# A gather shared out between four engines: 75 instead of 46 of 832 columns leave GpSimd, and their offsets shrink to 16 bits

## The reference

```python
x = x + _L0_gnn_ref(h, ...)   # GCN: sum over edges of H[src] * norm
x = x + _L1_gnn_ref(h, ...)   # SchNet: sum over edges of h[src] * filter(edge)
x = x + _L2_gnn_ref(h, ...)   # 4 EdgeConv layers: max over edges
x = x + _L3_gnn_ref(h, ...)   # GCN twice: sum over edges
```

## Time and profile before

| | us |
|---|---|
| median of 3 runs | 9450.62 (9448.05 to 9455.34) |
| the profiled execution | 9444.14 |
| its span | 9442.3 |
| GpSimd busy | 6987.7 (74%) |
| VectorE busy | 3654.1 (39%) |
| ScalarE busy | 3485.0 (37%) |
| TensorE busy | 1819.4 (19%) |

### The profile page before, as it was taken

One profiled execution on the slowest core, in us unless ns is written; L12 is line 12 of the kernel. 1 busy time (PEld: TensorE's weight loads), 2 busy tenths in 40 slices (PEclk: granted clock), 3 DMA queues, 4 the chain that ended last, 5 costly groups with the idle time before them and its releaser, 6 DMA issues. The chain is left out here.

```text
span 9442.3 us, 137452 instructions
## 1 busy us (share of the span) xinstructions
PE 1819.4 (19%) x9607; PEld 1531.1 (16%) x9607; DVE 3654.1 (39%) x20408; ACT 3485.0 (37%) x23810; POOL 6987.7 (74%) x6815
## 2 busy tenths in 40 slices
PE   2000057788884000020002000020002000020000
PEld 1000046777774000010001000010001000010000
DVE  4333344444443333333333333333334333333333
ACT  4444221111114444334442444334442444324441
POOL 5777668888883777777777777777776777777777
PEclk6555567777777555565556555565555555555555
DMA  6444535555553333333333333333334333333333
GB/s 214 161 159 158 190 79 77 77 77 77 75 72 111 108 108 112 110 108 108 113 111 111 111 109 108 113 105 112 108 110 138 103 117 111 109 108 110 108 112 128
DMA packets 483882, 1071.04 MB, mean 113 GB/s; under 512 B 162484, under 2 KB 293278, under 8 KB 428104
## 3 DMA queue, kind: packets, MB, share of 16 engines
q0 software_dynamic: 310432, 442.95, 21.5%
q1 hardware_dynamic: 169557, 619.06, 17.8%
q10 hardware_dynamic: 2940, 1.00, 0.1%
HBM read 511.83 MB, written 559.14 MB: 113 GB/s over the span
## 5 line engine op out<-in xcount | busy, mean ns | idle before, releaser
L1035 POOL DMA_INDIRECT WORK<-table,S x5502 | 5194.3, 944 | 1923.2 <-issue 1689.0
L1071 DVE COPY FE<-XF 128x4 uint8 x9856 | 1311.1, 190 | 3271.9 <-issue 1824.8
L1114 ACT COPY FE<-XF 128x4 uint8 x20608 | 2101.3, 191 | 1104.6 <-issue 1092.0
L1134 ACT COPY WORK<-psum 128x512 f32<-128x512 f32 (+1 forms) x1456 | 846.3, 581 | 2874.1 <-DVE psum L1089 2864.6
L1304 POOL DMA_INDIRECT acc<-TOT,stage x832 | 1301.3, 1564 | 274.6 <-issue 209.7
L1089 DVE SCALAR_TENSOR_TENSOR psum<-psum,RESET,WORK 128x128 f32<-128x128 f32 x3320 | 1189.1, 358 | 493.3 <-DMA WORK<-table,S 426.8
L1154 PE MATMUL psum<-ident,FE 128*128 128x128 f32 x238 | 106.5, 447 | 6110.0 <-ACT FE L1114 4714.0
L1089 DVE SCALAR_TENSOR_TENSOR psum<-psum,KEEP,WORK 128x128 f32<-128x128 f32 x2490 | 896.9, 360 | 639.9 <-DMA WORK<-table,S 278.8
L1154 PEld LDWEIGHTS psum<-ident,FE 128*128 128x128 f32 x238 | 43.3, 182 | 6172.5 <-issue 5903.0
L1438 ACT COPY TOT<-psum 128x512 f32<-128x512 f32 x208 | 121.9, 586 | 1250.2 <-DMA acc<-TOT,stage 1245.0
L1509 DVE SCALAR_TENSOR_TENSOR BASE<-psum,WEIGHT,BASE 128x128 f32<-128x128 f32 x832 | 234.1, 344 | 761.9 <-PE psum L1379 761.8
(11 more groups left out here) (255 smaller groups left out, 2540.4 us busy)
## 6 DMA issues: line engine op xcount, KB each, us to landing
run_rows<-WORK SPq DMA_DIRECT2D x357, 1024.0 KB, 4.2
WORK<-table SPq DMA_DIRECT2D x10752, 0.5 KB
WORK<-table,S POOLq DMA_INDIRECT x5502, 2.6
fill_rows<-BASE SPq DMA_DIRECT2D x52, 1024.0 KB, 6.8
WORK<-fill_rows SPq DMA_DIRECT2D x104, 512.0 KB, 3.7
table<-TF SPq DMA_DIRECT2D x56, 384.0 KB
WORK<-carry_rows SPq DMA_DIRECT2D x49, 384.0 KB, 6.6
acc<-TOT,stage POOLq DMA_INDIRECT x832, 3.3
```

Source lines behind the costliest of these rows:

```text
L1035: pool.indirect_dma_start(RING_T[:, b * WIDE + k, :], None, table, table_row(table, INDEX[:, t:t + 1]))\
L1071: i = dve.tensor_copy(PICKED[:, s, e:e + 1].bitcast(u8), TT[:, ds(held_rows["dve"][e % 32], 4)])
L1114: i = act.copy(PICKED[:, j % 2, e:e + 1].bitcast(u8), TT[:, ds(held_rows["act"][e % 32], 4)])
L1134: act.copy(RING_T[:, t % SPAN:t % SPAN + n, :], CHAINED[:, t % PSUM_COLS:t % PSUM_COLS + n, :])\
```

## The change

The shares and their places are new: ScalarE takes 36 columns, VectorE 24, SyncE 15. The offsets of ScalarE's and VectorE's columns are unsigned 16-bit numbers in `ROWB`; SyncE's stay 32 bits wide in a tensor of their own, `ROWS`. ScalarE picks a unit of 32 edges in three of four quads, VectorE 4 edges at each column. SyncE's columns lie at place 14 of chunks 3, 6, 9, 12, 16, 19, 22, 25, 28, 32, 35, 38, 41, 44 and 48; the halves are fetched behind the stores of chunks c-3 and c-2.

```diff
-BY_ACT = [t for t in range(60, 772, 32)]
-BY_DVE = [t for t in range(108, 772, 64)]
-BY_SP = [t for t in range(84, 800, 64)]
+UNIT = 32
+UNITS = P // UNIT
+TT_LAST = 800
+ACT_QUADS = [q for q in range(3, TT_LAST // QUAD) if q % 4 != 3]
+BY_ACT = [t for t in (QUAD * (q + 3) for q in ACT_QUADS[UNITS - 1::UNITS]) if t < TT_LAST]
+STEP_EDGES = 4
+DVE_STEPS = P // STEP_EDGES
+BY_DVE = list(range(DVE_STEPS + 3 * QUAD + 1, TT_LAST, DVE_STEPS))
+SP_BLOCKS = [c for c in range(3, TT_LAST // WIDE) if c % 16 in (3, 6, 9, 12, 0)]
+BY_SP = [WIDE * c + WIDE - 2 for c in SP_BLOCKS]
...
-EDGES = 16
-X_BLOCK = 48
-STEP_EDGES = 2
+X_BLOCK = 50
...
-        ROWB = sb("ROWB", [len(AWAY), P], i32)
+        ROWB = sb("ROWB", [len(FROM_TT), P], u16)
+        ROWS = sb("ROWS", [len(BY_SP), P], i32)
...
+                    if t < QUAD or j >= len(BY_DVE):
+                        return
...
+                    if first % UNIT == 0:
+                        offsets["dve"] = row_offsets(mybir.EngineType.DVE, ROWB, len(BY_ACT) + j, first // UNIT)
+                    for e in range(first, first + STEP_EDGES):
...
+                    rows = row_offsets(mybir.EngineType.Activation, ROWB, j, unit)
+                    for e in range(UNIT):
+                        i = act.copy(PICKED[:, j % 2, unit * UNIT + e:unit * UNIT + e + 1].bitcast(u8),
+                                     TT[:, ds(rows[e], 4)])
...
-                        k = after - max(c - RING, -1)
-                        parts_of = ((0, 64), (64, 64)) if c >= RING else ((0, 128),)
-                        if not 0 <= k < len(parts_of):
+                        half = after - (c - RING + 1)
+                        if half not in (0, 1):
                             continue
...
+                        wait(sp, stored[c % RING], c // RING * 16 if half == 0 else 0)
+                        for unit in range(half * UNITS // 2, (half + 1) * UNITS // 2):
+                            rows = row_offsets(mybir.EngineType.SP, ROWS, j, unit, 4 * F)
```

More of the change, by code:

```diff
@@ L83, in gnn_kernel @@
     f32, i32, u32, bf16 = mybir.dt.float32, mybir.dt.int32, mybir.dt.uint32, mybir.dt.bfloat16
-    u8 = mybir.dt.uint8
+    u8, u16 = mybir.dt.uint8, mybir.dt.uint16
     ALU = mybir.AluOpType
@@ L632, in _ @@
                                   ALU.is_equal).then_inc(hot, 1)
-                for k, (t, size) in enumerate([(t, 4) for t in BY_ACT + BY_DVE] + [(t, 4 * F) for t in BY_SP]):
-                    i = dve.tensor_single_scalar(AWAY_F[:, k:k + 1], SRCF[:, t:t + 1], float(size), ALU.mult)
+                k = 0
+                for cols_of, period, size in ((BY_ACT, 3, 4), (BY_DVE, 1, 4), (BY_SP, 5, 4 * F)):
+                    n = len(cols_of)
+                    for r in range(period):
+                        own = cols_of[r::period]
+                        assert own == list(range(own[0], own[-1] + 1, own[1] - own[0]))
+                        i = dve.tensor_single_scalar(AWAY_F[:, k + r:k + n:period],
+                                                     SRCF[:, own[0]:own[-1] + 1:own[1] - own[0]],
+                                                     float(size), ALU.mult)
+                    k += n
                 i.then_inc(hot, 1)
@@ L650, in _ @@
                 st.did(dve.memset(CHAIN[:], 0.0))
-                st.did(dve.tensor_copy(ROWB[:], bank(0)[0:len(AWAY), P:2 * P]))
+                st.did(dve.tensor_copy(ROWB[:], bank(0)[0:len(FROM_TT), P:2 * P]))
+                st.did(dve.tensor_copy(ROWS[:], bank(0)[0:len(BY_SP), 2 * P:3 * P]))
                 st.join()
@@ L743, in _ @@
                 pe.wait_ge(hot, 3)
-                nc.tensor.transpose(bank(0)[0:len(AWAY), P:2 * P], AWAY_F, ident[:])
+                nc.tensor.transpose(bank(0)[0:len(FROM_TT), P:2 * P], AWAY_F[:, 0:len(FROM_TT)], ident[:])
+                nc.tensor.transpose(bank(0)[0:len(BY_SP), 2 * P:3 * P], AWAY_F[:, len(FROM_TT):len(AWAY)], ident[:])
                 nc.tensor.matmul(bank(7)[:, 0:NT], upper[:], deg[:], start=True, stop=True)
@@ L995, in _, with row_offsets @@
                 wait(sp, x_parked, 16 * NG if x_loads == 1 else 0)
-        def row_offsets(engine, k, first, n, size=4):
+        def row_offsets(engine, rows, k, unit, size=4):
             return nc.values_load_multi_w_load_instructions(
-                ROWB[k:k + 1, first:first + n], engines=[engine], min_val=0, max_val=(N_PAD - 1) * size,
+                rows[k:k + 1, unit * UNIT:(unit + 1) * UNIT], engines=[engine], min_val=0,
+                max_val=(N_PAD - 1) * size,
                 skip_runtime_bounds_check_because="the offsets are made of node numbers below N_PAD")[1]
@@ L1024, in passing @@
             tt_quads = pieces(NT, QUAD) if FROM_TT else []
-            held_rows = {}
+            offsets = {}
             def pool_part(pool):
@@ L1059, in pick_edges @@
                 def pick_edges(t):
[L1060 to L1074, removed]
+                    j, first = divmod((t - QUAD) * STEP_EDGES, P)
+                    if t < QUAD or j >= len(BY_DVE):
+                        return
+                    s = 2 + j % 2
+                    if first == 0:
+                        wait(dve, tt_copied, len(tt_quads) if j == 0 else 0)
+                        wait(dve, off_turned, FROM_TT.index(BY_DVE[j - 2]) + 1 if j > 1 else 0)
+                    if first % UNIT == 0:
+                        offsets["dve"] = row_offsets(mybir.EngineType.DVE, ROWB, len(BY_ACT) + j, first // UNIT)
+                    for e in range(first, first + STEP_EDGES):
+                        i = dve.tensor_copy(PICKED[:, s, e:e + 1].bitcast(u8),
+                                            TT[:, ds(offsets["dve"][e % UNIT], 4)])
+                    if first + STEP_EDGES == P:
+                        i.then_inc(built_v, 1)
                 for t in range(T):
@@ L1104, in pick_edges @@
                 def pick_edges(q):
[L1105 to L1117, removed]
+                    if q not in ACT_QUADS:
+                        return
+                    j, unit = divmod(ACT_QUADS.index(q), UNITS)
+                    if j >= len(BY_ACT):
+                        return
+                    if unit == 0:
+                        wait(act, off_turned, FROM_TT.index(BY_ACT[j - 2]) + 1 if j > 1 else 0)
+                    rows = row_offsets(mybir.EngineType.Activation, ROWB, j, unit)
+                    for e in range(UNIT):
+                        i = act.copy(PICKED[:, j % 2, unit * UNIT + e:unit * UNIT + e + 1].bitcast(u8),
+                                     TT[:, ds(rows[e], 4)])
+                    if unit == UNITS - 1:
+                        i.then_inc(built_a, 1)
                 for q, (t, n) in enumerate(tt_quads):
@@ L1173, in fetch @@
                         c = col // WIDE
-                        k = after - max(c - RING, -1)
-                        parts_of = ((0, 64), (64, 64)) if c >= RING else ((0, 128),)
-                        if not 0 <= k < len(parts_of):
+                        half = after - (c - RING + 1)
+                        if half not in (0, 1):
                             continue
[L1178 to L1184, removed]
+                        wait(sp, stored[c % RING], c // RING * 16 if half == 0 else 0)
+                        for unit in range(half * UNITS // 2, (half + 1) * UNITS // 2):
+                            rows = row_offsets(mybir.EngineType.SP, ROWS, j, unit, 4 * F)
+                            for e in range(UNIT):
+                                p = unit * UNIT + e
+                                sp.dma_start(RING_T[p:p + 1, col % SPAN, :].bitcast(u8),
                                              flat_table[:, ds(rows[e], 4 * F)]).then_inc(fetched[j % 2], 16)
@@ L1188, in sp_part @@
                     sp.wait_ge(blanked, 1)
-                fetch(-1)
                 for c in range(COUNT):
```

## The result

The changed kernel takes **13774.01 us** (median of 4 runs, 13770.05 to 13775.10) against 9449.33 for the kernel before, run beside it: a ratio of 1.4575, 95% interval 1.4549 to 1.4600. The range for 8 in 10 ended at 9700.

What follows compares the result with a forecast made beforehand. SyncE's loop was taken to bound the kernel instead of GpSimd's gathers: six passes +14 us and the first +70, together +84 on 9444.14, with the median 6.5 above, gave 9535 us; own range 9470 to 9650, 8 in 10 from 9330 to 9700.

Steps and rivals of the forecast that it cites:

- halves: SyncE's 128 row loads per column, in two groups of 64 behind chunk stores: 27.8 us each from store to store.
- The range for 8 in 10: Total time of the changed kernel expected between 9330 and 9700 us with 8 in 10 confidence.
- the price of the 16-bit register load: ScalarE's load of 32 registers from 16-bit offsets: between 1.0 and 3.9 us, taken at 1.978.
- hidden: ScalarE's 16.4 us per 16 columns stay below GpSimd's 18.0, except three times a pass.
- Register loads make ScalarE the bound: Rival: past 3.1 us a load, ScalarE exceeds 19.5 us per chunk; at 3.9, some 10400 us in all. Chance 0.05.
- SyncE's loop: Store, half, store, half, landing, reduce, lift, next store, where SyncE's chunks stand three apart: 59.1 us for 48 columns.
- ordinary pass: Each of six passes after the first: last gather at 982.6 us against 980.3, so 2.3 us longer.
- the rest of the loop: From the end of SyncE's fetch through VectorE's reductions and ScalarE's lift to the store: 3.5 us.
- both register loads at 2.16: Rival, GpSimd stays the bound: SyncE's block at 56.4 us or less, pass 944, total 9198; chance 0.22 including a partial gain.
- GpSimd's step: Time from one GpSimd gather to the next: 1.2488 us, so 29 fewer gathers a pass save 36.2 us.
- 14 us of 18, hidden: VectorE's copies, reductions and two register loads in 16 columns take 14 us, within the 18 available.
- The signs: Profile observations that would show the forecast wrong: GpSimd's gathers gapless to 944, a SyncE half far from 27.8, register loads past 3 us.

Runs made afterwards that it cites:

- the 32-bit form: The changed kernel with all 75 rows of offsets as 32-bit numbers in one tensor, shares and places as changed: 9571.3 us, ratio 1.0143.
- the run with the load ahead: The 32-bit form with SyncE's first register load of each half made before it waits for the chunk and issues its store: 9284.46 us, ratio 0.9837.
- the spaced one: The 32-bit form with 12 SyncE columns, in every fourth chunk from 3 on, instead of 15; fetched behind the same stores: 9487.11 us, ratio 1.0052.

## Why the prediction was wrong

**The step that failed is the price of the 16-bit register load**, under *ScalarE*. It was bounded at 1.0 to 3.9 us and taken at 1.978, "since 32 registers are filled either way". It takes 7.1 (median 7.092), so 16 columns take ScalarE 32.2 us instead of 16.4, well above the 18.0 of GpSimd, and "hidden" fell with it. The bounds came from rows of another form of load: the lower by bytes, the upper by a load behind a store. Nothing in the trace of before had that width, so neither end was a bound. That the change came out slower, as forecast, doesn't bear the forecast out: the loop that it rests on makes the 32-bit form 136 us slower, and lies beneath ScalarE's loads in the change itself.

**The rival had the right mechanism at 0.05.** "Register loads make ScalarE the bound" gives, by its own formula with 7.1 put in, 3 x (7.1 + 3.15) + 0.8 = 31.6 us per 16 columns, and 27 + 48.5 x 31.6 + 23 = 1583 us a pass. Measured were 32.2 us on average and 1572: the formula's step is 0.6 us short and it counts some one step too many, which partly cancel. It was given 0.05 because I let one row overrule a stated price. The Trainium skill, Runtime: NRT & Kernel Launch, section on instruction fetch mechanics, has about 200 ns a register for loads from HBM. The 16-bit loads from SBUF here cost 6718 / 32 = 210 ns each, the aligned 32-bit ones 1964 / 32 = 61 ns. The trace of before spoke only of the second kind. With a price of the Trainium skill at hand for a form that no row showed, 6.4 us belonged into the range.

**SyncE's loop** was right: 59.1 us forecast, 59.7 in the 32-bit form. There an ordinary pass is 986 to 988 us, 982.6 forecast; the first 1088.8, 1079 forecast; the whole 9571 against 9535. Its parts were right too: halves of 28.0 to 28.2 for 27.8, and so 3.6 us for the rest of the loop, 3.5 forecast. The rival's "both register loads at 2.16" comes close to the run with the load ahead: a loop of 56.7 us for its 56.4, and 948 us a pass for its 944.

**GpSimd's step** was right: 759 steps of 1.2488 us where nothing else binds. **VectorE** at "14 us of 18, hidden", holds at 32 bits alone; with 16-bit loads on VectorE only, it binds at 1260 us a pass.

**The signs** named beforehand, register loads past 3 us as one that the prediction is wrong, came true in the first view.

## What to carry to other kernels

Price an instruction by its own form: a change of element type is a new instruction, though the count of registers is the same, and a price from another form bounds nothing. Offsets for bulk register loads are best kept as 32-bit numbers here, from a start that four divides; halving the bytes made the load 3.4 times as long. Where a queue's store and fetch alternate, see which of the next chunk's waits lie inside the loop: moving a load ahead of the store took 287 us off the 32-bit form, and the fetch one store earlier 284 off the spaced one, where the spacing itself, with three columns back on GpSimd, gave 84.

## What the runs showed of the hardware

- A register load of 32 numbers from SBUF on ScalarE takes 1.96 us at 32 bits and 6.72 at 16; on VectorE the same forms take 2.1 and 7.1.
- On ScalarE five 32-bit registers (0.538 us) cost less than three (0.702). From element 1 or 2 of the row, 32 cost 6.8 us, from 0, 4, 8 or 16 they cost 1.96.
- In the 32-bit form a register load of 32 numbers begun within 2 us of a 1 MB store's issue takes about 4 us instead of 2, on SyncE, ScalarE and VectorE. On SyncE the first row load then comes 4.77 us behind the store, and 0.45 with the register load made ahead; the row loads behind the store reach 1.011 us, against 0.387 at most.
